# A state-space and attention layer on one core: values of two head groups in one visit, real products shared between ScalarE and VectorE, and new orders for all queues

## The reference

```python
# h = Re sum_n Wc[c,h,n] * exp(dt_Lambda[h,n] * l),  l = 0..1023   -> (64, 128, 1024)
K = jnp.einsum('chn,hnl->chl', Wc, jnp.exp(P)); h = K.real
# attention: 32 heads of 32, 8 key/value heads, RoPE, causal softmax
q, k, v = x @ Wq, x @ Wk, x @ Wv
attn = softmax(mask(rope(q) @ rope(k).T / sqrt(32)))
h = h + (attn @ v) @ Wo                       # on layernorm(h)
# mixture: 8 experts of rank 16, weights 8 * softmax(x @ Wr + br), scaled by 2
h = h + 2 * einsum('bshr,hor,bsh->bso', x @ A, B, scores)   # on layernorm(h)
```

## Time and profile before

| | before |
|---|---|
| median of 3 runs | 2622.91 us (2618.62 to 2625.13) |
| the profiled execution | 2622.32 us |
| its span, first to last instruction | 2620.3 us |
| TensorE busy | 2394.3 us, 91% of the span |
| VectorE busy | 2110.4 us, 81% |
| ScalarE busy | 1922.0 us, 73% |
| GpSimd busy | 1700.8 us, 65% |
| DMA, share of 16 engines' span | 85.2% |

### The profile page before, as it was taken

How to read it: one execution, slowest core, us unless ns; L and a number is a source line. 1 busy time by engine, 2 the same in 40 slices (tenths; PEclk the granted TensorE clock), 3 DMA queues, 4 the chain that set the end, 5 groups by cost and what they waited for, 6 DMA issues and landing times.

```text
span 2620.3 us, 59857 instructions
## 1 busy us (share of the span) xinstructions
PE 2394.3 (91%) x18752; PEld 1236.4 (47%) x18752; DVE 2110.4 (81%) x8162; ACT 1922.0 (73%) x6782; POOL 1700.8 (65%) x1508
## 2 busy tenths in 40 slices
PE   2777679999999999999999999999999999999985
PEld 2666534444444444444444444444444444444442
DVE  7888548888888888888888888888888888888873
ACT  5888647777777777777777777777777777777772
POOL 1232147777777777777777777777777777777771
PEclk9999889999999999999999999999999999999997
DMA  2677558999999899999989898989999999999983
GB/s 74 205 201 201 161 101 162 168 175 175 181 181 175 170 178 172 168 174 181 182 179 174 174 176 172 170 173 178 184 171 177 177 175 170 169 178 179 184 149 81
DMA packets 1199532, 443.70 MB, mean 169 GB/s; under 512 B 1149552, under 2 KB 1151856, under 8 KB 1199216
## 3 DMA queue, kind: packets, MB, share of 16 engines
q1 hardware_dynamic: 1199216, 439.89, 85.2%
HBM read 87.42 MB, written 67.11 MB: 59 GB/s over the span
## 4 chain that ended last, share of the span: by engine, by line
PE 38%; DMA 15%; DVE 13%; POOL 9%; issue 5%; ACT 4%; SPq 3%; ACTq 0%; DVEq 0%; POOLq 0%
DMA pt<-p 7%; PE pb L807 5%; PE pb L809 4%; PE pb L808 4%; DVE xs L1159 4%; PE pa L807 4%; POOL p L1323 4%; DMA xt<-xs 4%; PE pa L808 4%; PE pa L809 4%; POOL pr L1315 3%; PE pv_ps L834 3%; DVE pr L1106 2%; DMA x2t<-xs 2%; PE s_ps L821 2%
## 5 line engine op out<-in xcount | busy, mean ns | idle before, releaser
L960 ACT ACTIVATE pr<-pr,smin 128x128 f32<-128x128 f32 x2048 | 793.1, 389 | 117.3 <-DVE smin L1106 117.2
L1323 POOL TENSOR_TENSOR p<-pr,p 128x512 f16<-128x512 f32 x512 | 619.4, 1214 | 252.2 <-ACT p L970 251.7
L1315 POOL TENSOR_TENSOR pr<-pr,rinv 128x512 f32<-128x512 f32 x512 | 562.2, 1098 | 317.9 <-DVE rinv L1114 315.8
L1106 DVE CUSTOM_DVE_ANT_0 pr<-s_ps,cst 128x128 f32<-128x128 f32 x2048 | 469.8, 284 | 60.6 <-POOL p L1323 50.9
L970 ACT ACTIVATE p<-pr 128x512 f16<-128x512 f32 x512 | 320.0, 625 | 250.6 <-POOL pr L1315 174.4
L960 ACT ACTIVATION_READ_ACCUMULATOR pr<-pr,smin 128x1 f32 x2048 | 385.1, 188 | 0.0
L566 PE MATMUL hps<-z,xw 128*128 128x256 f32 x896 | 214.3, 400 | 94.1 <-issue 47.0
L1120 DVE TENSOR_TENSOR ctx_t<-pv_ps,ctx_t 128x128 f16<-128x128 f32 x512 | 144.6, 282 | 134.0 <-ACT ctx_t L978 128.1
L807 PE MATMUL pa<-wkv_hi,xt 128*128 128x512 f16 x512 | 194.8, 380 | 49.1 <-DMA xt<-xs 48.5
L566 PEld LDWEIGHTS hps<-z,xw 128*128 128x128 f32 x896 | 177.7, 201 | 130.4 <-issue 104.5
L978 ACT ACTIVATE ctx_t<-pv_ps 128x128 f16<-128x128 f32 x512 | 138.2, 270 | 128.7 <-PE pv_ps L834 125.3
(11 more groups left out here) (187 smaller groups left out, 6183.6 us busy)
## 6 DMA issues: line engine op xcount, KB each, us to landing
h<-hout SPq DMA_DIRECT2D x128, 256.0 KB, 3.2
h_ln<-h SPq DMA_DIRECT2D x64, 512.0 KB, 4.9
h_res<-h SPq DMA_DIRECT2D x64, 512.0 KB, 4.3
out<-h SPq DMA_DIRECT2D x64, 512.0 KB, 3.2
pt<-p SPq DMA_TRANSPOSE x512, 3.4
xa<-x SPq DMA_DIRECT2D x16, 256.0 KB, 4.3
xb<-x SPq DMA_DIRECT2D x32, 128.0 KB, 4.0
wst<-wq SPq DMA_DIRECT2D x8, 512.0 KB, 5.4
```

What stands on the lines that cost most here:

```text
L960: last = A.activation(p, p, ACT.Exp, bias=smin[g % 2][:, j:j + 1], scale=-1.0, accum_out=rsum[g % 2][:, j:j + 1])
L1106: V.tensor_tensor_reduce(pr[g % 2][:, cols], s_ps[g % 2][:, cols], mask, 1.0, 3e38, ALU.add, ALU.min, smin[g % 2][:, j:j + 1]).then_inc(ma ...
L1315: nc.gpsimd.tensor_tensor(p3, p3, rinv[g % 2][:, :].unsqueeze(2).broadcast_to([P, HG, P]), ALU.mult).then_inc(p_norm, 1)
L1323: nc.gpsimd.tensor_tensor(p[:, HG * P:], pr[g % 2][:, :], p[:, 0:HG * P], ALU.subtract).then_inc(pl_done, 1)
```

## The change

First stage: ScalarE makes the real products of three tokens of each window (`ON_ACT = 3`), three windows ahead instead of two (`LEAD = 3`). The fourth token's four products are one 128x256 instruction on VectorE, in `swapped`, from a copy of `top_r` that is laid into PSUM (`top_p`). The key/value weights are due in the last window of a chunk, the two single pieces one window earlier than before, and the high part of `wq` is made one window ahead of its low part. In the first window, `swapped(1)` comes behind the tables.

Layer stage: `values`, `ctx_high` and `ctx_low` take two groups (256 columns of `pv_ps`); their semaphores count to 4 a block instead of 8. The bodies of all five engines are written in a new order, and `out_half`, the second residual and the store belong to block i-3.

```diff
+LEAD = 3
+ON_ACT = 3
...
-            PIECES += [(4 * k + 1, "wq", k, D, 1), (4 * k + 1, "wo", k, D, 1), (4 * k + 2, "wkv", k, 512, 2)]
+            PIECES += [(4 * k + 1, "wq", k, D, 1), (4 * k + 1, "wo", k, D, 1)]
             if k < 2:
-                PIECES.append((4 * k + 3, ("aw", "bm")[k], None, (KC * AW, D)[k], 1))
+                PIECES.append((4 * k + 2, ("aw", "bm")[k], None, (KC * AW, D)[k], 1))
+            PIECES.append((4 * k + 3, "wkv", k, 512, 2))
...
-                    if e == WIN - 1:
+                    if e == ON_ACT - 1:
                         last.then_inc(pr_done, 1)
...
+                    for n, piece in enumerate(PIECES):
+                        if w == (piece[0] - 1 if piece[1] == "wq" else piece[0]):
+                            weight_hi(n)
                     for e in range(WIN):
-                        if w + 2 < WINDOWS:
-                            products(w + 2, e)
+                        if e < ON_ACT and w + LEAD < WINDOWS:
+                            products(w + LEAD, e)
                         evict(WIN * w + e)
...
-                                    top_i3[:, t:t + WIN, :].unsqueeze(3).broadcast_to([P, WIN, TOPS, NB]),
+                                    top_i3[:, t:t + WIN, :].unsqueeze(3).broadcast_to([P, WIN, TOPS, NB]), ALU.mult)
+                    if w >= XWR:
+                        dve.wait_ge(tok_done, WIN * (w - XWR) + WIN)
+                    rest, n = slice(t % XT + ON_ACT, t % XT + WIN), WIN - ON_ACT
+                    V.tensor_tensor(xw[w % XWR][:, ON_ACT:, :, :],
+                                    xa[slot][:, rest, :].unsqueeze(2).broadcast_to([P, n, TOPS, NB]),
+                                    top_p3[:, t + ON_ACT:t + WIN, :].unsqueeze(3).broadcast_to([P, n, TOPS, NB]),
                                     ALU.mult).then_inc(pi_done, 1)
...
+                step(V.tensor_copy(top_p3.rearrange("p t q -> p q t"), top_r[:, :, :]))
...
-                def values(b, g, odd):
+                def values(b, m, odd):
...
-                    reached(pe, ctxl_done, G, b, g)
-                    for n, (v, lo) in enumerate(((v_hi[odd], 0), (v_lo[odd], 0), (v_hi[odd], HG))):
-                        for j in range(HG):
-                            last = pe.matmul(pv_ps[j * HD:(j + 1) * HD, 0:P], v[:, g * HD:(g + 1) * HD],
-                                             pt[g % RP][:, lo + j, :], start=(n == 0), stop=(n == 2))
+                    reached(pe, ctxl_done, G // 2, b, m)
+                    for g in (2 * m, 2 * m + 1):
+                        landed(pe, b, g)
+                        to = slice(P * (g % 2), P * (g % 2) + P)
+                        for n, (v, lo) in enumerate(((v_hi[odd], 0), (v_lo[odd], 0), (v_hi[odd], HG))):
+                            for j in range(HG):
+                                last = pe.matmul(pv_ps[j * HD:(j + 1) * HD, to], v[:, g * HD:(g + 1) * HD],
+                                                 pt[g % RP][:, lo + j, :], start=(n == 0), stop=(n == 2))
                     last.then_inc(pv_done, 1)
...
+                    wo_half(i - 1, 1 - odd, 0, 5, 8)
+                    values(i, 1, odd)
...
+                    kv(i + 2, odd, 0, 2)
+                    wo_half(i - 1, 1 - odd, 1, 6, 8)
```

More of the change, by code:

```diff
@@ L354, in _ @@
                 act.wait_ge(pre_v, V_T)
-                for w in range(2):
-                    for e in range(WIN):
+                for w in range(LEAD):
+                    for e in range(ON_ACT):
                         products(w, e)
@@ L911, in body @@
[L911 to L919, removed]
-                    values(i, 1, odd)
-                    wo_half(i - 1, 1 - odd, 1, 2, 4)
@@ L922, in body @@
-                    wo_half(i - 1, 1 - odd, 0, 2, 5)
-                    wo_half(i - 1, 1 - odd, 1, 4, 5)
-                    wo_half(i - 1, 1 - odd, 0, 5, 7)
+                    q_half(i + 1, 1 - odd, 1, 0, 1)
+                    q_half(i + 1, 1 - odd, 0, 5, 6)
+                    scores(i, 3)
+                    q_half(i + 1, 1 - odd, 1, 1, 2)
+                    q_half(i + 1, 1 - odd, 0, 6, 8)
+                    q_half(i + 1, 1 - odd, 1, 2, 5)
+                    wo_half(i - 1, 1 - odd, 0, 0, 1)
@@ new lines, in body @@
+                    wo_half(i - 1, 1 - odd, 1, 0, 1)
+                    scores(i, 4)
+                    out_half(i - 3, 0)
+                    wo_half(i - 1, 1 - odd, 1, 1, 2)
+                    wo_half(i - 1, 1 - odd, 0, 1, 2)
+                    out_half(i - 3, 1)
+                    q_half(i + 1, 1 - odd, 1, 5, 6)
+                    values(i - 1, 3, 1 - odd)
+                    wo_half(i - 1, 1 - odd, 1, 2, 3)
+                    scores(i, 5)
+                    wo_half(i - 1, 1 - odd, 0, 2, 4)
@@ new lines, in body @@
+                    wo_half(i - 1, 1 - odd, 1, 3, 5)
+                    scores(i, 6)
+                    wo_half(i - 1, 1 - odd, 0, 4, 5)
+                    values(i, 0, odd)
+                    low(i - 2)
+                    wo_half(i - 1, 1 - odd, 1, 5, 6)
+                    q_half(i + 1, 1 - odd, 1, 6, 7)
+                    wo_half(i - 1, 1 - odd, 0, 5, 8)
+                    values(i, 1, odd)
+                    q_half(i + 1, 1 - odd, 1, 7, 8)
+                    scores(i, 7)
@@ L925, in body @@
+                    kv(i + 2, odd, 0, 2)
+                    wo_half(i - 1, 1 - odd, 1, 6, 8)
+                    kv(i + 2, odd, 2, 5)
+                    scores(i + 1, 0)
+                    q_half(i + 2, odd, 0, 0, 2)
+                    kv(i + 2, odd, 5, 6)
                     ls_transpose(i - 2)
[L926 to L929, removed]
+                    scores(i + 1, 1)
@@ L930, in body @@
+                    kv(i + 2, odd, 6, 7)
+                    scores(i + 1, 2)
+                    q_half(i + 2, odd, 0, 2, 5)
                     values(i, 2, odd)
[L931 to L945, removed]
+                    kv(i + 2, odd, 7, 8)
                 bodies(pe, body)
@@ L1290, in body @@
[L1290 to L1297 removed]
+                    ctx_low(i - 1, 2, 1 - odd)
+                    x_low(0, i + 2, 0)
+                    mask_min(i, 4)
+                    residual2(i - 3, 0, 1 - odd)
@@ new lines, in body @@
+                    ctx_low(i - 1, 3, 1 - odd)
+                    x_low(0, i + 2, 1)
+                    reciprocals(i, 4)
+                    residual2(i - 3, 1, 1 - odd)
+                    mask_min(i, 5)
+                    router_max(i - 2)
+                    mask_min(i, 6)
+                    ctx_low(i, 0, odd)
+                    q_double(i + 1, 0)
+                    reciprocals(i, 5)
+                    reciprocals(i, 6)
+                    residual1(i - 1, 0, 1 - odd)
+                    q_rotate(i + 1, 1)
```

179 lines of the change are left out of this document (72 added, 107 removed).

## The result

The change takes 2504.69 us (median of 4 runs, 2504.22 to 2505.99) against 2624.02 us for the kernel before: a ratio of 0.955, 95% interval 0.9533 to 0.9566. The forecast was 2526 us in a range of 2480 to 2592, so the sign, the size and the range held. The profiled execution spans 2502.4 us, 117.9 less than before. Its parts came out otherwise than forecast.

A forecast was written before the change was run, and what follows sets the result against it. VectorE's list was taken to set the first stage, TensorE's own work the steady layer stage. The terms -36 - 49 - 14 + 3 = -96 us on 2622.3 gave 2526 us, range 2480 to 2592 us.

The forecast's parts named there:

- Two groups in one visit: Layer stage, `values`: 256 pairs of TensorE weight switches at 0.19 us go, -49 us, bounds -45 to -51.
- New order: Layer stage: earlier transpose of `xt` shrinks TensorE's waits, -14 us, bounds -50 (nearly all waits go) and +110.
- I take a quarter off: Layer stage: of TensorE's 0.91 us without work per block, 0.23 us goes, times 64 blocks, -14 us.
- rival B: Layer stage: VectorE late at `mask_min(i+1, 0)`, for which a score group waits; slower, 2649 us at 1.7 us per block; chance 0.09.
- First stage, -36 us: First stage: moved weights and fewer held instructions, less VectorE's new instruction, shorten it by 36 us, bounds -10 and -50.
- I take all 39.3 us off VectorE: First stage: weights moved by a window end VectorE's waits for high parts of `wkv` and `wo`; bounds 25 and 39.
- So VectorE's list sets this stage: First stage: VectorE's busy time, 39.3 us of waits and small gaps make 259 of the 270 us.
- The other two terms: First stage, VectorE: 18 us less from instructions held by GpSimd's add, and 13.8 us more for the new instruction.
- Fill and drain, +3 us: Layer stage's fill and drain: a block's last steps come half a period later, +3 us, bounds -5 and +15.
- D: First stage alone fails, held by stores or TensorE's clock: -10 us, 2552 us; sign: over 255 us; forecast including this 0.62.
- C: Layer stage: nearly all TensorE waits go, period 33.0 us, 2475 us in all; chance 0.12.
- Rival A: Layer stage: softmax chain or transfers hold the old period and give back what `values` saves, 2589 us; chance 0.17.

The follow-up runs named there:

- e3: The change with each two-group visit to `values` cut in two by three 512-column products: 2557.08 us, 0.973 of the kernel before.
- e11: The kernel before with `values`, `ctx_high` and `ctx_low` for two groups at the odd groups' places, other orders unchanged: 2593.89 us, ratio 0.9894.
- e12: The change with ScalarE two windows ahead instead of three (`LEAD = 2`): 2503.53 us, 0.9549 of the kernel before.
- e6: The change with three output buffers `hout` instead of two in the first stage (`HR = 3`): 2489.32 us, 0.9491 of the kernel before.
- e8: The change with all real products on ScalarE again (`ON_ACT = 4`), no product on VectorE: 2514.19 us, 0.9587 of the kernel before.
- e7_xt_late: The change with the transpose `xt` put back behind groups 4 and 5 of `pt` on SyncE's list: 3046.24 us, 1.162 of the kernel before.

## Why the prediction was right, and where it was not

*Two groups in one visit, -49 us: right.* The 0.19 us read from one visit times 256 is what e3 gave back, 47 us by the ratios and 54 by the period. The condition, that nothing else takes its place, holds in the new order only; e11 has 28 us of it.

*New order, -14 us: right in sign and place, far too small.* The period fell by 1.52 us, of which the visits are 0.75 to 0.84; the other 0.68 to 0.77 us a block are 44 to 49 us, the far bound. TensorE's stops by the starts fell by the same, from 1.09 to 0.42 us. The step that failed is "I take a quarter off". The waits I feared did come, at the score group named in rival B and at the rotation, but cost TensorE only 0.25 and 0.17 us a block and took the place of larger ones. This share is a remainder, what is left beside the visits; how much each moved item gave to it is not shown.

*First stage, -36 us: too large, it was -13.5.* The step that failed is "I take all 39.3 us off VectorE". I read the wait as one for a late load, with ScalarE in between. The load of `wkv` came in time and the wait stayed at 41 us: 30 of it since ScalarE's list was the later one, which follows TensorE and the stores, and 11 for `aw` and `bm`, made due too early by the change itself. Behind this step stands a premise that failed too, "So VectorE's list sets this stage": VectorE had 13 us more to do in e12 and as much to do in e6, while the stage stayed as it was in the one and became 13.3 us shorter in the other. Nor is ScalarE's relief "worth nothing by itself": e8, which takes it back, is slower although VectorE has less to do. The limit by stores I named, and left 7.5 us for it together with the nearness of TensorE; e6 puts the stores, with the clock, at 13 us. (The sum also slips by 2 us: VectorE's 259 us have become 261 where the savings are taken off.) The other two terms were right as lengths on VectorE's list, though by e12 the first was worth nothing to the stage. The excess of held instructions fell from 27 to about 5 us (14 x 0.07 on L460, 7 x 0.16 on L392, and 3 us on two other groups), a little more than the 18 us I took and near the 21 that the shared-port rule of the Trainium skill ("SBUF — State Buffer", section "Who interferes with whom") gave. The trace agrees with that rule, but 18 and 21 are too near each other for it to choose. The new instruction takes 0.41 us, for 0.43.

*Fill and drain, +3 us: they were -7.* No run shows why.

The total, -96 against -118 us of span, is near because the first stage's miss (+22) and the order's (-30 to -35) point opposite ways, with -10 from fill and drain. That is luck. The two stages followed two different rivals: the first went as D had it, with 256.7 us and ScalarE waiting 29.8 us for stores, which was my own sign of being wrong; the layer stage went nearly as C had it, with a period of 33.20 us against its 33.0. Rival A had the transfers as a limit at a share of 0.95: at 0.96 and a period of 33.20 us they did not hold the old period.

## What to carry to other kernels

A wait names the instruction that came last, not the reason why it was late: before counting it as gained, ask what stands in front of the releasing instruction on its own list. Where TensorE is the limit, count how often it changes between weight widths, as each round trip costs work that no wait shows. A new order of one queue is only right beside the orders of the others; judge them together, and expect single swaps to move a wait rather than remove it.

## What was unexpected in the hardware

In `e7_xt_late` TensorE's mean granted clock in the steady stretch was 0.91 with stops of 6.7 us a block, against 1.00 in every other run. The mean is made of two levels, 2.4 and 1.2 GHz: between 1000 and 1090 us the three stretches of 10 us that hold a stop have 0.66 to 0.69, the six others 1.00. In the first stage it rose from 0.94 to 0.97 when only the stops for stores went (e6), which shortened its busy time from 213 to 206 us. The stops thus cost twice, once by themselves and once in slower matmuls.

An instruction of VectorE on one column of four bytes can be held like a large one: the 128x1 step L1144 of the norm takes 543 ns in the mean in the change's steady stretch, where the same step (L1138) took 211 before. In this place it ends with the GpSimd instruction that ran when it began:

```profile
1035.71 1.04 POOL L1317 TENSOR_TENSOR pr<-pr,rinv 128x512 f32<-128x512 f32 x1
```
```profile
1036.02 0.75 DVE L1144 SCALAR_TENSOR_TENSOR nrm<-nrm 128x1 f32<-128x1 f32 x1
```
